# A graph network's first stage: projecting raw node tiles by chunks, and finding each node's edges from sign marks and TensorE products

## What is computed

```
h = layernorm(x)                                   # over the 256 values of a node
xh = (h @ W).reshape(N, 8, 32)
a_src, a_dst = (xh * att_src).sum(-1), (xh * att_dst).sum(-1)      # 3125 x 8 each
e = leaky_relu(a_src[src] + a_dst[dst], 0.2)       # per edge, and one loop per node
alpha = softmax of e over the edges of one dst
out = segment_sum(xh[src] * alpha, dst) + bias, batch norm over the nodes, + h
```

## Time and profile before

| | us |
|---|---|
| median of three runs | 1977.33 |
| the profiled execution, its own time | 1977.53 |
| its span, from the first to the last instruction | 1975.8 |
| PE busy | 1365.6 (69%) |
| POOL busy | 1098.3 (56%) |
| DVE busy | 907.3 (46%) |
| ACT busy | 576.3 (29%) |

### The profile page before, as it was taken

How to read it: one execution, slowest core, us unless ns; L and a number is a source line. 1 busy time by engine, 2 the same in 40 slices (tenths; PEclk the granted TensorE clock), 3 DMA queues, 4 the chain that set the end, 5 groups by cost and what they waited for, 6 DMA issues and landing times. The chain is left out here.

```text
span 1975.8 us, 23808 instructions
## 1 busy us (share of the span) xinstructions
PE 1365.6 (69%) x6688; PEld 1134.1 (57%) x6688; DVE 907.3 (46%) x1818; ACT 576.3 (29%) x1264; POOL 1098.3 (56%) x1086
## 2 busy tenths in 40 slices
PE   2435666656666266599999997656666666567998
PEld 2324544444454146599999997444445444346787
DVE  7425544444443667633333333644334333335953
ACT  2133433323333014133333332422222222222310
POOL 4477777777774600377222273077777777773520
PEclk7756878878878575699999999877878787978999
DMA  6484998888887601432111122743333333330002
GB/s 145 119 251 150 298 312 284 281 285 272 276 283 258 155 6 63 134 115 83 46 46 46 46 98 65 174 142 104 105 105 105 105 104 105 106 99 1 1 1 65
DMA packets 156809, 268.56 MB, mean 136 GB/s; under 512 B 26747, under 2 KB 119839, under 8 KB 155567
## 3 DMA queue, kind: packets, MB, share of 16 engines
q1 hardware_dynamic: 100252, 135.75, 22.1%
q0 software_dynamic: 46224, 123.97, 21.0%
q10 hardware_dynamic: 10213, 7.36, 1.5%
HBM read 169.82 MB, written 98.15 MB: 136 GB/s over the span
## 5 line engine op out<-in xcount | busy, mean ns | idle before, releaser
L1182 POOL DMA_INDIRECT sum_rows<-xn_tab,src_e x391 | 373.3, 955 | 174.5 <-issue 118.8
L1207 PE MATMUL bank<-sum_held,sum_hot 128*125 128x256 f32 x976 | 304.1, 474 | 195.3 <-ACT sum_held L1217 191.1
L798 POOL DMA_INDIRECT gat_rows<-xh_tab,src_e x363 | 343.4, 946 | 114.8 <-issue 107.8
L1207 PEld LDWEIGHTS bank<-sum_held,sum_hot 128*125 128x125 f32 x976 | 222.2, 236 | 273.5 <-issue 179.7
L871 PE MATMUL bank<-gat_rows,gat_same 128*128 128x264 f32 x784 | 263.7, 483 | 126.2 <-issue 126.2
L871 PEld LDWEIGHTS bank<-gat_rows,gat_same 128*128 128x128 f32 x784 | 176.6, 244 | 166.4 <-issue 132.6
L1217 ACT COPY sum_held<-sum_rows 128x1024 f32 x122 | 127.4, 1045 | 373.6 <-SPq L1173 334.1
L1894 PE MATMUL bank<-weights,e_xthigh 128*128 x896 | 220.3, 330 | 8.5 <-DVE e_xtlow L2049 5.4
L915 ACT COPY gat_outs<-bank 128x528 f32<-128x528 f32 x196 | 117.3, 598 | 281.8 <-PE bank L871 280.5
L2054 DVE TENSOR_TENSOR e_h<-e_gated,bank 128x342 f32<-128x342 f32 x112 | 57.1, 510 | 262.9 <-ACT e_gated L1987 262.9
L1239 DVE SCALAR_TENSOR_TENSOR res<-bank,prep_inv,res 125x256 f32 x122 | 58.9, 483 | 234.8 <-PE bank L1207 228.2
(11 more groups left out here) (508 smaller groups left out, 2416.8 us busy)
## 6 DMA issues: line engine op xcount, KB each, us to landing
parts<-gat_outs SPq DMA_DIRECT2D x27, 1904.0 KB, 8.0
staged<-w_tab SPq DMA_DIRECT2D x8, 2132.0 KB, 8.9
w_tab<-w_stage SPq DMA_DIRECT2D x16, 682.0 KB, 10.6
w_raw<-in_L_ffn_w_dram SPq DMA_DIRECT2D x16, 640.0 KB
gat_rows<-xh_tab,src_e POOLq DMA_INDIRECT x391, 4.7
sum_rows<-xn_tab,src_e POOLq DMA_INDIRECT x391, 2.8
w_tab<-w_stage SPq DMA_DIRECT2D x8, 768.0 KB, 10.6
weights<-y_tab SPq DMA_DIRECT2D x10, 600.0 KB
```

The source lines that it names most:

```text
L798: pool.indirect_dma_start(out=rows[b % R][:, t, :], out_offset=None, in_=k.xh_tab, in_offset=bass.IndirectOffsetOnAxis(ap=k.src_e[:, b * S ...
L1182: pool.indirect_dma_start(out=rows[:, at // IP % (RING * GPAIRS), at % IP, :], out_offset=None, in_=k.xn_tab, in_offset=bass.IndirectOffse ...
L1207: m = nc.tensor.matmul(k.ps[s][0:P, 0:C], hot[g % 2][:, s, c, :], held[:, s, c, :], start=(c == 0), stop=(c == IP - 1))
```

## The change

What it does, part by part:

- SP issues x in five chunks of five tiles right behind the edge lists, each with its own semaphore, then `bias` (from ScalarE's queue), the zeros for `adst_edge` and the row `dummy`; then all stores of `xh_tab`, and after them all of `adst_tab`. `dst_pad` and `start_tab` and their DMAs go.
- The tiles are transposed raw. The mean is taken out through the weights: PE sums each column of `w` over its 256 rows, and VectorE subtracts a 256th of the sum from `w`. The division by the deviation is one multiplication in the take, which is now `(bank * rstd) + bias`. Statistics and roots are made chunk by chunk.
- The starts come from products. ScalarE makes `passed` from a row of the node numbers: for each of the 392 edge tiles the sign of node minus the tile's first target, for all 3125 nodes (four activations over 98 partitions). VectorE makes `rises`: for each edge tile, how much each of its 128 targets is above the target in the same place one tile before, and a column of ones. Four products of PE, added up in PSUM over the 392 edge tiles, give for each of 125 nodes twice the targets of its own edge tile, less a constant, and in the 129th column the place of that tile. Then VectorE and ScalarE count the targets below the node, two tiles of four each. The ends come from two small products with a shifted identity.
- The copies of the edge columns come after the work on `w`. `joins` moves to `Walk.on_vector` and `shift` is made from the statistics.

The diff, cut to its core:

```diff
         def _(sp):
-            sp.wait_ge(edges_f, 1)
-            sp.dma_start(k.dst_pad.rearrange("(q e) -> q e", q=Q), dstq[:, :]).then_inc(pad_out, 16)
-            move(sp, k.res[:, :, :], k.a["x"].rearrange("(t p) c -> p t c", p=P), x_in)
+            for c in range(CHUNKS):
+                move(sp, k.res[:, c * TB:(c + 1) * TB, :], x_rows[:, c * TB:(c + 1) * TB, :], x_in[c])
+            sp.dma_start(bias[:, 0:C], k.a["L0_gnn_bias"].rearrange("(a c) -> a c", a=1).to_broadcast([P, C])).then_inc(bias_in, 16)
...
+            for c in range(CHUNKS):
+                tiles = slice(c * TB, (c + 1) * TB)
+                sp.wait_ge(taken, (c + 1) * TB)
+                move(sp, xh_rows[:, tiles, :], k.xh[:, tiles, 0:XW], xh_done)
+            for c in range(CHUNKS):
+                tiles = slice(c * TB, (c + 1) * TB)
+                move(sp, adst_rows[:, tiles, :], k.xh[:, tiles, XW:RW], adst_out)
...
         def _(act):
+            act.dma_start(prev_i[1:Q, :], k.a["dst"][0:(Q - 1) * J * EP].rearrange("(q e) -> q e", e=J * EP)[:, (J - 1) * EP:J * EP]).then_inc(prev_in, 16)
+            act.wait_ge(eps_made, 1)
+            nc.scalar.activation(root0[:, :], eps[:, :], ACT.Sqrt)
+            act.wait_ge(numbered, 1)
+            act.wait_ge(firsts_made, 1)
+            for j in range(J):
+                nc.scalar.activation(passed[:, j, :], node_row, ACT.Sign, bias=neg_first[:, j:j + 1]).then_inc(passed_made, 1)
+            for c in range(CHUNKS):
+                for t in range(c * TB, (c + 1) * TB):
+                    act.wait_ge(xt_turned, t + 1)
+                    if t >= XR:
+                        act.wait_ge(projected, t - XR + 1)
+                    nc.scalar.copy(xt[:, t % XR, :, :].rearrange("p a n -> p (a n)"), k.ps[t % XR][:, 0:2 * P]).then_inc(xt_made, 1)
+                    if t % TB == 2:
+                        act.wait_ge(deviations, c + 1)
+                        nc.scalar.activation(k.rstd[:, c * TB:(c + 1) * TB], spread[:, c * TB:(c + 1) * TB], ACT.Sqrt, bias=eps[:, 0:1], scale=1.0 / C).then_inc(roots, 1)
+            act.wait_ge(halves_made, 1)
+            for t in range(NT):
+                if t % WG >= BY_DVE:
+                    act.wait_ge(windows, t + 1)
+                    nc.scalar.activation(trash[:, t % 8, :], k.ps[t % 8][0:P, 0:EP], ACT.Sign, bias=half[:, t:t + 1], scale=-1.0,
+                                         accum_out=before[:, t:t + 1]).then_inc(signed, 1)
...
         def _(pool):
+            nc.gpsimd.iota(node_row, pattern=[[1, N]], base=0, channel_multiplier=0, allow_small_or_imprecise_dtypes=True).then_inc(numbered, 1)
-            for t in range(NT):
-                pool.indirect_dma_start(out=windows[:, t, :], out_offset=None, in_=k.dst_pad.rearrange("(a b) -> a b", b=EP),
-                                        in_offset=bass.IndirectOffsetOnAxis(ap=tiles_i[:, t:t + 1], axis=0)).then_inc(windows_in, 16)
...
         def _(pe):
+            pe.wait_ge(w_whole, 1)
+            for c in range(2):
+                last_mm = nc.tensor.matmul(k.ps[XR - 1][:, 0:RW], k.ones[:, :], w[:, c, :], start=(c == 0), stop=(c == 1))
+            last_mm.then_inc(w_summed, 1)
+            for t in range(NT + 1):
+                if t < NT:
+                    if t == XR - 1:
+                        pe.wait_ge(w_ready, 1)
+                    if t % TB == 0:
+                        pe.wait_ge(x_in[t // TB], 32)
+                    if t >= XR:
+                        pe.wait_ge(xt_made, t - XR + 1)
                     for c in range(2):
+                        last_mm = nc.tensor.transpose(k.ps[t % XR][:, c * P:(c + 1) * P], k.res[:, t, c * 128:(c + 1) * 128], k.ident[0:P, 0:P])
                     last_mm.then_inc(xt_turned, 1)
+                if t:
+                    u = t - 1
+                    pe.wait_ge(xt_made, u + 1)
+                    if u == 0:
+                        pe.wait_ge(w_ready, 1)
+                    if u < XP:
+                        pe.wait_ge(columns_made, u + 1)
+                    else:
+                        pe.wait_ge(taken, u - XP + 1)
                     for c in range(2):
+                        last_mm = nc.tensor.matmul(k.ps[XR + u % XP][0:P, 0:RW], xt[:, u % XR, c, :], w[:, c, :], start=(c == 0), stop=(c == 1))
                     last_mm.then_inc(projected, 1)
+            pe.wait_ge(passed_made, J)
+            pe.wait_ge(rises_made, 1)
+            for t in range(NT):
+                g = t // WG
+                if g < 2:
+                    pe.wait_ge(taken, NT if g else NT - XP + 1)
+                else:
+                    pe.wait_ge(tiles_kept, g - 1)
+                for j in range(J):
+                    last_mm = nc.tensor.matmul(k.ps[t % 8][0:P, 0:WIN], passed[:, j, t * P:(t + 1) * P], rises[:, j, :], start=(j == 0), stop=(j == J - 1))
+                last_mm.then_inc(windows, 1)
...
         def _(dve):
+            for c in range(2):
+                m = v.scalar_tensor_tensor(out=w[:, c, :], in0=k.ps[XR - 1][:, 0:RW], scalar=-1.0 / C, in1=w[:, c, :], op0=ALU.mult, op1=ALU.add)
+            m.then_inc(w_ready, 1)
+            for b, t in enumerate((k.dst_e, k.src_e, k.fwd_e, k.bwd_e, k.seat_e)):
+                dve.wait_ge(turned, b + 1)
...
+            dve.wait_ge(prev_in, 16)
             dve.wait_ge(bias_in, 16)
+            for c in range(CHUNKS):
+                if c < CHUNKS - 1:
+                    spreads(c + 1)
+                take(c)
+                if c == 2:
...
+                    v.memset(rises[0:1, 0, EP:WIN], 0.0).then_inc(rises_made, 1)
```

More of the change, by code:

```diff
@@ L216, in first_phase @@
[L216 to L224, removed]
@@ L285, in _ @@
-            norm_roots(k, act, deviations, roots)
-            act.sem_inc(xt_made, TB)
-            xh_rows = k.xh_tab.rearrange("(t p) c -> p t c", p=P)
-            def store(i):
-                act.wait_ge(taken, (i + 2) * TB)
-                move(act, xh_rows[:, i * TB:(i + 1) * TB, :], k.xh[:, i * TB:(i + 1) * TB, 0:XW], xh_done)
-            for i in range(NT // TB):
-                for s in range(TB):
-                    act.wait_ge(xt_turned, i * TB + s + 1 + TB)
-                    act.wait_ge(projected, i * TB + s + 1)
-                    nc.scalar.copy(xt[:, s, :, :].rearrange("p a n -> p (a n)"), k.ps[s % 3][:, 0:2 * P]).then_inc(xt_made, 1)
-                if i:
-                    store(i - 1)
@@ new lines, in take @@
+            def take(c):
+                rstd = k.rstd[:, c * TB:(c + 1) * TB]
+                dve.wait_ge(roots, c + 1)
+                me(dve, v.reciprocal(rstd, rstd))
+                for t in range(c * TB, (c + 1) * TB):
+                    dve.wait_ge(projected, t + 1)
+                    v.scalar_tensor_tensor(out=k.xh[:, t, :], in0=k.ps[XR + t % XP][0:P, 0:RW], scalar=k.rstd[:, t:t + 1], in1=bias[:, :], op0=ALU.mult, op1=ALU.add).then_inc(taken, 1)
+            spreads(0)
+            dve.wait_ge(w_summed, 1)
@@ new lines, in _ @@
+            marked = lambda n: n // WG * BY_DVE + min(n % WG, BY_DVE)
+            for g in range(GROUPS):
+                ahead = min((g + 1) * WG, NT)
+                for t in range(g * WG, min(g * WG + BY_DVE, NT)):
+                    dve.wait_ge(windows, t + 1)
+                    v.tensor_scalar(trash[:, t % 8, :], k.ps[t % 8][0:P, 0:EP], below[:, t:t + 1], None, ALU.is_lt, ALU.add, accum_out=before[:, t:t + 1]).then_inc(counted, 1)
+                dve.wait_ge(counted, marked(ahead))
+                dve.wait_ge(signed, ahead - marked(ahead))
+                v.tensor_scalar(tile[:, g * WG:ahead], k.banks[0:P, g % 2 * WG:g % 2 * WG + ahead - g * WG, EP], 0.5 * EP, 0.5 * EP * (ET - 1), ALU.mult, ALU.add).then_inc(tiles_kept, 1)
@@ new lines, in _ @@
+            signs = before[:, 0:NT // WG * WG].rearrange("p (c s) -> p c s", s=WG)[:, :, BY_DVE:WG]
+            dve.wait_ge(tiles_kept, GROUPS)
+            me(dve, v.tensor_scalar(signs, signs, 0.5, 0.5 * EP, ALU.mult, ALU.add))
+            v.tensor_tensor(start[:, 0:NT], tile[:, :], before[:, :], ALU.add).then_inc(starts_made, 1)
+            dve.wait_ge(starts_made, 1)
+            me(dve, v.tensor_scalar(t0[:, :], start[:, 0:NT], -float(NO_ROW + 1), None, ALU.add))
+            dve.wait_ge(ends_made, 1)
@@ L465, in _ @@
+            end = k.ps[0][0:P, 0:NT]
+            v.tensor_scalar(last[:, :], end, -1.0, 0.0, ALU.add, ALU.max)
+            me(dve, v.tensor_tensor(k.deg[:, :], end, start[:, 0:NT], ALU.subtract))
+            me(dve, v.tensor_scalar(has[:, :], k.deg[:, :], 0.0, None, ALU.is_gt))
             me(dve, v.tensor_tensor(t0[:, :], t0[:, :], has[:, :], ALU.mult))
             me(dve, v.tensor_scalar(k.start_row[:, :], t0[:, :], float(NO_ROW + 1), None, ALU.add))
+            me(dve, v.scalar_tensor_tensor(out=last[:, :], in0=last[:, :], scalar=-float(NO_ROW), in1=has[:, :], op0=ALU.add, op1=ALU.mult))
```

237 lines of the change are left out of this document (85 added, 152 removed).

## The result

The changed kernel takes 1954.5 us (median of 4 runs, 1951.1 to 1957.49) beside 1976.35 of the kernel before (4 runs, 1971.5 to 1977.82): a ratio of 0.9887, interval 0.9867 to 0.9907, 21.9 us less. That is on the side that was forecast and under the range, whose low end was 1956. The profiled execution took 1957.49, its span 1955.7.

A forecast was written before the change was run, and what follows sets the result against it. It took the first stage's end to be bound by last tile, stores and POOL's fourteen gathers: 57.6 + 6.3 + 20.9 = 84.8 against 100.6, so -15.8 of 1977.53, forecast 1961.7 us, range 1956 to 1970.

The forecast's parts named there:

- the crossing: Passage from first to second stage, at the issue of `w_raw`; forecast at 84.8 against 100.6 before.
- (3): Rival for the new products: bank hand-over between PE and two counting engines stretches each to 0.30; 1967.8 us, chance 0.06.
- (4): Rival for the new products: they run at 1.2 GHz, making the kernel slower, 1984.3 us; chance 0.06.
- (5): Rival: the gain is given back, something behind POOL being late instead; 1977 us, chance 0.04.
- S: First stage, when the takes begin, at the statistics of chunk 1; forecast at 28.5.
- 30.8 - 3.5 + 1.2: Sum for the takes' beginning: today's landing of x, less its earlier issue, plus `bias`, `prev_i` and W loads sharing the time.
- rival (1): Rival for the takes' beginning: `bias` lands early, VectorE's work alone decides, 24.6; 1957.8 us, chance 0.12.
- Rival (2): Rival for the takes' beginning: narrow transfers are late, `prev_i` holding one engine 4 us, 32.5; 1965.7 us, chance 0.12.
- The ramp of 1.2: Projection of the tiles: PE's first turn after a long rest takes 1.2 us more, added to twenty tiles' time.
- The turn of 6.03: Projection of the tiles: PE takes 6.03 us for five tiles at 2.4 GHz, four such turns for twenty tiles.
- 20.9: End of the first stage: 20.9 us for POOL's fourteen gathers and the passage into the second stage.
- wins nothing by itself: Claim that removing counts, signs, window gathers and `dst_pad`, which lay beside x's landing, gains nothing alone.

The follow-up runs named there:

- before_x_early: The kernel before the change, with SP issuing x ahead of its wait for the cast edge lists; ratio 1.0011.
- bias_on_act: The changed kernel with the `bias` load moved to ScalarE's queue behind the two `att` loads; 1953.18 us, ratio 0.9875.
- bias_and_prev: The changed kernel with `bias` on ScalarE's queue and `prev_i` fetched as 96 rows and one; ratio 0.988, on a slower chip.
- prev_split: The changed kernel with `prev_i` fetched in 96 rows and one instead of 97 at once; ratio 0.9905, on a slower chip.
- turns_of_three: The changed kernel with PE transposing three tiles, then making the products of the three before; 1958.14 us, ratio 0.9906.
- x_after_edges: The changed kernel with SP waiting for `edges_f` before it issues x, as in the kernel before; 1961.71 us, ratio 0.992.
- idle_gathers_spread: The changed kernel with 25 unused indirect gathers added in POOL's wait, each row from another place of x; 1954.5 us in two runs.
- after_third: The changed kernel unedited, run again on a slower chip; 2304.37 us, ratio 0.9898.
- idle_gathers: The changed kernel with 25 unused indirect gathers added in POOL's wait, all reading one row of x; ratio 0.9971, on a slower chip.

## Why the prediction was wrong, and where it was right

**Right** was the chain. POOL's fourteen gathers end the stage; the stores behind the last take cost 6.19 for 6.3, and each gather still 1.25; the products cost 0.223 each at 2.4 GHz and stay hidden, by 1 us where I had 1.6; the second stage moves with the crossing, within 1.3 us; none of rivals (3), (4) and (5) came true on the ordinary chips. On the slower ones the products do end the stage, by gaps that none of the rivals had.

**The step that failed is S**, "30.8 - 3.5 + 1.2". I shifted today's landing by the earlier issue alone. All of x had landed by 24.55, so its load ended at least 6.2 us earlier, not 3.5. The step takes today's load over whole, and its last 6 us were a tail, of which the earlier trace rows shows the end. The windows of the kernel before (DMA share next to last):

```profile
22.00:24.00 2.00, 0.00 (x0) 0.00 (x0) 2.00 (x9) 1.92 (x4) 0.00 (x0) 0.50 1.06 190
24.00:26.00 2.00, 0.00 (x0) 0.00 (x0) 2.00 (x9) 0.00 (x0) 0.00 (x0) 0.50 0.67 136
26.00:28.00 2.00, 0.00 (x0) 0.00 (x0) 1.82 (x7) 0.00 (x0) 1.08 (x1) 0.50 0.31 63
```

before_x_early, which also loads x in one `move`, has such a tail too (0.47, 0.34 and 0.10 in the three windows from 22 to 28) and had x by 27.74. So the early issue alone was worth 3.0, close to my 3.5, and the other 3.2 came with the five chunks, as far as two chips can be compared. Why chunks end sooner was not tried. The wait I named was the right one, `bias` (bias_on_act), but it ended at 25.8. This is between the forecast and rival (1), whose 24.6 for VectorE's own work was itself too high: that work is done at 22.4 (bias_and_prev). VectorE began on W at 13.06, not 14.1; five copies in a row take 3.6 instead of 4.3, and the four small operations 0.6 instead of 0.8, since neighbours overlap by their ends. Rival (2)'s mechanism is likely, but smaller than its 4 us: some 1.5 for `bias` (prev_split), and `prev_i` itself there at 24.1 (bias_on_act).

**Mis-sized were three more terms**, all on one side. The ramp of 1.2: PE's work ahead of S had already borne it, under VectorE's copies. I had added it after S without asking what PE does before. It wasn't safe to leave out either: in turns_of_three, x_after_edges and idle_gathers_spread, and in after_third with the kernel unedited, PE had its five tiles done sooner, rested 2.6 to 5.7 us and did pay. The turn of 6.03: it was read from a kernel that groups its transposes by five, and the diff alternates them; 5.68, four times 0.35, is 1.4. And the crossing: 20.9 was carried over whole, though the 25 window gathers that the change removes were in it; 1.07, shown by idle_gathers_spread, less some 0.2 for the first gather being longer. I had written that their going "wins nothing by itself".

Together 2.7 + 1.2 + 1.4 + 0.8, and 0.4 in the ends: 6.5. Each was inside its own bounds or nearly, and I had taken the slow side four times; on its lower side the range allowed for an error of S and for none of the others.

## What to carry to other kernels

When a chain is moved, ask of each piece that you carry over whole what the change took out of it: a turn read off another order of instructions, and a block's end that had 39 indirect DMAs in it and now has 14, were both wrong by a microsecond. The slow start was paid here where PE first worked; under another engine's work it was free, but a rest behind it brought it back. A load of an awkward number of rows, such as 97, can delay its neighbours too: split off the odd row, and put small loads that gate a loop ahead of the large one. When a load is moved, look at the DMA share of its last microseconds first: a tail need not move with it.

## What the runs showed of the hardware

- Gathers whose descriptors all name one row are slow: of the DMA queues' packets in idle_gathers, 800 of the indirect queue took 64.0% of 16 engines over 52 us, 0.67 us each; with spread rows 800 took 6.0% over 50 us, 0.06 each. The two ran on different chips.
- Indirect DMAs issued long before, and landed, still cost some 0.04 us each at the end of the block in which POOL issued them.
- The granted clock's column can read 1.00 at the start of a span, while products take twice their time.
- On two of the chips PE's issue stumbles after some 140 rows of back-to-back fp32 products, and in before_x_early, on one of them, ScalarE made no copy for 19.56 us in the projection. With that, the gain depends on the chip in its place (products or gathers last), though hardly in its ratio: 0.9898 there (after_third), 0.9887 and 0.9891 on the others.
